# One core of Trainium2: VectorE reads a flag and three split numbers ahead of the last edge sums, scales sums three tiles ahead, and biases one layer-3 product inside a group's statistics

## What is computed

```python
xn = layernorm(x)
def conv(h, rel, W_in, W_out, W_loop, b):          # twice, h -> h + res * conv(h)
    m = h[src] * rel[edge_type]
    m = concat([m[:E//2] @ W_in, m[E//2:] @ W_out])
    norm = 1 / maximum(segment_sum(ones, dst), 1)
    return tanh(segment_sum(m * norm[dst], dst) + h @ W_loop + b)
x = x + (conv twice, then @ mu_w + mu_b)(xn) + four_transformer_layers(xn)
out = x + shared_mlp(layernorm(x)) + top2_of_4_experts(layernorm(x))
```

## Time and profile before

| | |
|---|---|
| median of 3 runs | 1995.1 us (1994.89 to 1996.6) |
| profiled execution: its time | 1993.74 us |
| profiled execution: its span | 1992.1 us |
| TensorE / its weight loads busy | 1846.9 us (93%) / 1514.1 us (76%) |
| VectorE / ScalarE / GpSimd busy | 1250.1 us (63%) / 629.9 us (32%) / 1334.6 us (67%) |
| mean granted TensorE clock | 0.984 of full speed |
| HBM traffic over the span | 186 GB/s |

### The profile page before, as it was taken

The page is one execution under the profiler, slowest core; times in us unless marked ns, Lnnn a source line. Parts: engine busy times, 40 slices in busy tenths (PEclk is TensorE's granted clock), DMA queues, the critical chain, the costliest instruction groups (busy, mean ns, idle before and its releaser), DMA issues.

```text
span 1992.1 us, 29170 instructions
## 1 busy us (share of the span) xinstructions
PE 1846.9 (93%) x9216; PEld 1514.1 (76%) x9216; DVE 1250.1 (63%) x3324; ACT 629.9 (32%) x1544; POOL 1334.6 (67%) x1326
## 2 busy tenths in 40 slices
PE   3889999999799999989999989987999999999999
PEld 1557887787587887767888777665888887888998
DVE  6786564674655665575576555577666566663866
ACT  4441243343222343332343233221121221222433
POOL 6777777777777777777777614776777777771000
PEclk9999999999899999999999999989999999999999
DMA  9668667667766666677666635677666667662101
GB/s 274 189 199 256 197 188 205 197 187 225 229 206 204 190 196 205 189 246 228 203 187 200 209 88 193 198 232 209 205 201 209 199 201 208 198 186 45 24 23 31
DMA packets 194574, 371.43 MB, mean 186 GB/s; under 512 B 37993, under 2 KB 126095, under 8 KB 194430
## 3 DMA queue, kind: packets, MB, share of 16 engines
q0 software_dynamic: 77632, 223.91, 39.5%
q1 hardware_dynamic: 92228, 126.68, 19.3%
q10 hardware_dynamic: 24570, 19.04, 3.3%
HBM read 305.39 MB, written 64.95 MB: 186 GB/s over the span
## 4 chain that ended last, share of the span: by engine, by line
PE 67%; DVE 10%; POOL 10%; issue 6%; DMA 4%; SPq 2%; ACT 1%; DVEq 1%; ACTq 0%
PE ps_seg L2542 13%; PE ps_down L2668 12%; PE ps_hid L2656 12%; POOL xg L919 7%; PE ps_kv L2575 4%; PE ps_x L2620 3%; POOL rg L870 3%; PE ps_hid L3132 2%; DVE xg L1021 2%; PE ps_x L531 2%; PE ps_x L2986 2%; DMA xg<-h_rows,idx_tab 2%; PE ps_kv L2986 2%; PE ps_hid L2595 1%; PE ps_kv L2696 1%
## 5 line engine op out<-in xcount | busy, mean ns | idle before, releaser
L919 POOL DMA_INDIRECT xg<-h_rows,idx_tab x416 | 435.0, 1046 | 141.0 <-issue 117.7
L919 POOL DMA_INDIRECT xg<-xn_rows,idx_tab x416 | 431.3, 1037 | 129.6 <-issue 121.6
L870 POOL DMA_INDIRECT rg<-relation_rows,idx_tab x416 | 428.6, 1030 | 133.7 <-issue 126.5
L2542 PE MATMUL ps_seg<-xg,hot 128*125 128x257 f32 x1664 | 428.0, 390 | 52.1 <-DVE xg L1021 51.8
L2542 PEld LDWEIGHTS ps_seg<-xg,hot 128*125 128x125 f32 x1664 | 305.4, 190 | 125.2 <-DVE xg L1021 51.1
L2656 PE MATMUL ps_hid<-hT,wff 128*128 128x250 f32 (+1 forms) x1920 | 371.7, 341 | 0.9 <-issue 0.9
L2668 PE MATMUL ps_down<-wff,gT 128*125 128x256 f32 x1600 | 364.9, 381 | 0.0
L1021 DVE TENSOR_TENSOR xg<-xg,rg 128x512 f32<-128x512 f32 x416 | 285.1, 685 | 104.9 <-DMA xg<-h_rows,idx_tab 54.6
L2656 PEld LDWEIGHTS ps_hid<-hT,wff 128*128 128x128 f32 x1920 | 315.5, 190 | 38.4 <-issue 7.0
L2668 PEld LDWEIGHTS ps_down<-wff,gT 128*125 128x125 f32 x1600 | 296.2, 189 | 41.8
L2126 ACT ACTIVATE gT<-ps_hid,b1p 128x250 f32<-128x250 f32 (+1 forms) x480 | 178.2, 434 | 320.9 <-PE ps_hid L2656 318.6
(11 more groups left out here) (364 smaller groups left out, 2390.9 us busy)
## 6 DMA issues: line engine op xcount, KB each, us to landing
second_relation_rows<-rg SPq DMA_DIRECT2D x104, 512.0 KB, 4.0
rg<-second_relation_rows SPq DMA_DIRECT2D x104, 512.0 KB, 4.0
wff<-L_mix_W ACTq DMA_DIRECT2D x8, 1024.0 KB, 6.3
rg<-relation_rows,idx_tab POOLq DMA_INDIRECT x416, 3.6
xg<-xn_rows,idx_tab POOLq DMA_INDIRECT x416, 3.3
xg<-h_rows,idx_tab POOLq DMA_INDIRECT x416, 3.7
rg<-xn_rows SPq DMA_DIRECT2D x25, 112.0 KB
h_rows<-rg SPq DMA_DIRECT2D x25, 112.0 KB
```

Of the source, the lines that this page charges most:

```text
L870: pool.indirect_dma_start(rg[:, k, :], None, rel_d, bass.IndirectOffsetOnAxis(ap=idx_tab[:, step, 1:2], axis=0))\
L919: pool.indirect_dma_start(xg[:, k, 0:D], None, rows, bass.IndirectOffsetOnAxis(ap=idx_tab[:, step, 0:1], axis=0))\
L2542: ins = pe.matmul(ps_seg[u // UW % 2][0:T, 0:AW], hot[:, s % HOTS, :], xg[:, s % RING, :], start=s % WIN == 0, stop=s % WIN == WIN - 1)
```

## The change

It moves work of VectorE's queue; no instruction of another engine changes.

1. In layer 2, group 3, the three split numbers are read, and then the flag, before `flush` adds the last window; `general` takes the flag's register as an argument. In layer 3, group 0, the flag is read just ahead of a wait instead of just behind it.
2. `dense_head` scales the rest and tiles 0, 1 and 2, and tile t then scales tile t + 3 instead of t + 2. The four buffers stay.
3. In layer 3's groups 0 to 3 `aside(5)` is issued behind the first unit inside `n.stats`, between the five `bn_stats` and the five `bn_aggr`. Group 4 keeps its place.

```diff
-                def stats(self, between, beside=lambda j: None):
+                def stats(self, between, behind_unit=lambda: None):
                     def rows(j):
-                        beside(j)
                         hold(dve, s_xa, self.tn + (j + 2))
                         return self.row(j)
-                    stats_of("b", self.lay, self.gi, rows, between)
+                    pieces = [behind_unit]
+
+                    def unit_and_piece():
+                        between()
+                        if pieces:
+                            pieces.pop()()
+                    stats_of("b", self.lay, self.gi, rows, unit_and_piece)
...
-                    n.stats(lambda: one(m["down2"] + 1 if dense_behind(lay, gi) else m["up4"] - 1))
+                    n.stats(lambda: one(m["down2"] + 1 if dense_behind(lay, gi) else m["up4"] - 1), lambda: aside(5))
...
-                aside(5)
+                if not n:
+                    aside(5)
...
                 if dense_behind(lay, gi):
                     upto(m["end"])
-                    sums_done()
+                    self_split.read()
+                    sums_done(any_unsorted())
...
+            def any_unsorted():
+                return dve.value_load(unsorted_i[0:1, 0:1], min_val=0, max_val=1)
+
-            def general(g):
+            def general(g, unsorted):
...
-                with dve.If(dve.value_load(unsorted_i[0:1, 0:1], min_val=0, max_val=1) == 1):
+                with dve.If(unsorted == 1):
...
                 dd(dve.tensor_tensor(deg2, deg[1], in_second, ALU.mult))
-                self_split.read()
                 dd.wait()
...
-                scale_tile(0)
-                scale_tile(1)
+                for t in range(SLOTS - 1):
+                    scale_tile(t)
...
-                    if t + 2 < NT:
-                        scale_tile(t + 2)
+                    if t + SLOTS - 1 < NT:
+                        scale_tile(t + SLOTS - 1)
...
-                    def sums_done():
+                    def sums_done(unsorted):
                         edges.flush()
-                        general(0)
+                        general(0, unsorted)
...
-                        general(1)
+                        general(1, any_unsorted())
```

## The result

| | before | after |
|---|---|---|
| median of 11 runs | 1994.89 us (1986.55 to 1996.6) | 1984.0 us (1978.73 to 1991.11) |
| profiled execution: time / span | 1993.74 / 1992.1 us | 1987.24 / 1985.6 us |
| mean granted TensorE clock | 0.984 | 0.987 |

After stands to before as 0.9959, with a 95% interval of 0.9945 to 0.9974: 8.2 us less, between 5.2 and 11.0. The forecast was 8.2 us less. The forecast for the median was 1986.9 us and 1984.0 were measured, 0.6 us inside the lower end of the range. By the median alone the layer-3 rival (1983.6) would fit better, so the sections of the two profiles have to decide.

The account below looks back on a forecast made before the run. The prediction took the chain of waits into the dense part, through VectorE with register loads, and TensorE's waits there as the bound, with gathers pacing layer 3. 2.2 + 1.7 + 4.2 + 0.1 = 8.2 us: median 1986.9, range 1983.4 to 1991.3.

Parts of the forecast that it names:

- layer-3 rival: Layer 3: GpSimd isn't the pace, TensorE's time there counts in full; 11.5 us won, 1983.6; chance 0.10.
- Part 1, the reads: Ahead of the dense part: register loads leave the chain of waits; 2.2 us won, bounds 0.4 to 2.25.
- Just in time: Before the last window's sum: the four moved loads end at 1148.5, when the sum is released; 0.05 us late taken.
- Part 1, the clock: First transpose to tile 2's: without the wait TensorE's clock should not fall; 1.7 us won, bounds 0 to 1.74.
- Part 2, the lead: Dense part: scaling three tiles ahead removes TensorE's stalls for scaled sums; 4.2 us won, bounds 3.2 to 4.3.
- k_shift's: Dense part: this 0.86 us stall moves to a longer wait for ScalarE's copy of tile 8, near 2 us; nothing won.
- Part 3, the bias: Layer 3: TensorE saves 3.36 us of waits, but gathers set the pace; 0.1 us won, bounds 0 to 3.36.
- what it wins at 1715 meets rows at 1785 that were ready 0.1 us before: Layer 3, group 3: TensorE's saved bias wait runs into gathered rows ready 0.1 us before use; 0.1 us taken.
- The time of layer 3 counts in full: Rival for layer 3: GpSimd isn't the pace, so 11.5 us are won, 1983.6; chance 0.10.
- The reads come late: Rival ahead of the dense part: reads pile up behind busy VectorE, half-speed stretch stays; 5.5 us won, 1989.6; chance 0.14.
- The lead doesn't do what it says: Rival in the dense part: stalls pass to ScalarE's copies; only part 1's 3.9 us won, 1991.2; chance 0.12.
- SyncE did not become the bound: Judges the slower rival: SyncE's queue becomes the bound in the dense part, 2005; chance 0.03.

Follow-up runs that it names:

- e_bias2: The kernel before with part 3 alone (dense bias inside the next group's statistics); ratio 0.9999 to the kernel before, median 1990.63 us.
- e_pe_early: The changed kernel with TensorE's product for the result matrix computed twice for tiles 0 to 5 (layer 3's groups 0 and 1); 1987.84 us in one execution.
- e_pad4: The changed kernel with four more loads of the flag, values unused, ahead of the one that counts; 1999.58 us in one execution.
- e_pe_late: The changed kernel with the product for the result matrix computed twice for tiles 14 to 19 (layer 3's group 3); 1986.56 us, ratio 0.9986 to the kernel before.
- e_table2: The changed kernel with one exponential of a single number ahead of ScalarE's first copy of the dense part; 1981.91 us, ratio 0.9944 to the kernel before.

## Why the prediction was right

**Part 1, the reads: right.** 2.2 us forecast, 2.24 and 2.25 measured, and the four loads took 0.30 us each. "Just in time" was close: 0.4 us of room. It comes from the load that the prediction had at 0.87 us, the row number's, which now stands behind the others and took 0.30 (at 1151.7 of the profile after).

**Part 1, the clock: right in its place, too sure of its size.** The half-speed stretch went with the wait. But the 1.7 us were read from one profile. The four profiles with that wait lost 1.67, 1.67, 1.24 and 0 us: 1.15 on average is what removing it is worth. The step that failed is the upper bound taken as the value, on the ground that shorter waits had left the clock alone; it should have asked as well whether this wait always brings it down.

**Part 2, the lead: the working held, one term was missing.** All waits for scaled sums went, and k_shift's passed to ScalarE's copy, 1.99 us long where "near 2 us" was forecast. Without a fall of the clock it won 59.53 - 55.17 = 4.36 us, forecast 4.23. The 1.6 us that the prediction gives VectorE's ordinary work in a tile were too many (in before, bias, update and scaling take 1.14 us from 1209.36 to 1210.50), which erred on the safe side. What was missing is that a wait of 2 us can do here what the one of 2.30 us did at the start. The prediction took that step in part 1 and not in part 2. It costs 1.7 us in half of the profiles, among them the one of after, where part 2 won 2.68 us, below the range of 3.2 to 4.3, so that it is worth about 4.36 - 0.84 = 3.5 us on average.

**Part 3, the bias: right for groups 0 and 1, wrong for group 3.** 0.1 us forecast, 1.3 measured in group 3, inside the bounds of 0 to 3.36. That GpSimd issues gathers until 1800 was right, and after shows the same (its gathers from 1221.3 to 1794.9, before from 1223.6 to 1799.4). The step that failed is "what it wins at 1715 meets rows at 1785 that were ready 0.1 us before": between 1660 and 1795 gathers are not what TensorE waits for, but VectorE's queue, and that moves along with TensorE. The rows at 1785 were late indeed: VectorE waited 2.76 us for them in before and 3.21 in after, but TensorE in neither, and the last gather starts 47.2 us behind the second long wait in before and 47.5 in after, so the gathers came earlier as well. What ties them to it isn't shown. The trace of before showed it: the longest wait there, 3.34 us at 1661.81, had VectorE busy right through it, with the end of the norm at 1659.00 and no wait for a DMA at the multiplication that released TensorE:

```profile
1659.00 1.70 DVE L1735 TENSOR_SCALAR acc<-xres,mv,rstd 125x256 f32<-125x256 f32 x5
...
1661.07 0.69 DVE L1021 TENSOR_TENSOR xg<-xg,rg 128x512 f32<-128x512 f32 x1
```

**The rivals.** "The time of layer 3 counts in full" is refuted by the profiles of e_bias2 and e_pe_early; the times alone don't exclude it. "The reads come late" is refuted as a fact and shown as a mechanism by e_pad4: with four loads more it happens. "The lead doesn't do what it says" came true for one of seven stalls only, as forecast. SyncE did not become the bound: VectorE has no wait for stored rows in the dense part, and a store and a load follow each other there in 2.2 us.

**The sum.** 2.25 + 1.15 + 3.5 + 1.3 = 8.2 us by the averages of all profiles, against the forecast's 2.2 + 1.7 + 4.2 + 0.1 = 8.2 and 8.2 measured. That they agree to the tenth is luck: three terms were off by 0.6, 0.7 and 1.2 us and cancel, the averages come from four and six profiles, and the measurement's own interval is 5.8 us wide. What holds is the mechanism of parts 1 and 2; that of part 3 was wrong in group 3.

## What to carry to other kernels

Here a wait of about 2 us on TensorE had two prices, its length for certain and a half-speed stretch in some profiles and not in others; weigh the second by how often it happened over several profiles, and ask for it also at a wait that the change itself makes longer. When a wait names the operation that releases it, look at what that engine did before: if it was busy, its queue's order made the wait, and that moved along with TensorE here; if it was idle, a transfer did, and that didn't. The load of a table that a function of ScalarE needs can be put where ScalarE is idle, with that function of a single number.

## What the runs showed of the hardware

Nearly equal waits of TensorE brought the granted clock down in seven of eleven cases: three of four at 2.3 us (by 1.67 us twice, by 1.24 once), the one of 2.06 us in e_pad4 (by 1.65), and three of six at 1.98 to 1.99 us (by 1.68 each). Waits of 1.10 us at tile 8 did so in none of four, waits of 0.56 us in none of four. I know no sign in the profile that tells the cases apart. And a product behind 20 matmuls of 4 columns ran at half speed for most of its time in before, e_pe_early and e_pe_late (5.38 us) and at full speed in after, e_bias2, e_pad4 and e_table2 (3.70 us), without any wait.
